# Unit 0, its handover to unit 1, and the last unit rearranged: first keys in three passes, film rows spread by TensorE, low value halves shared

## What is computed

```
xn  = layernorm(x) * ln_w + ln_b
q   = softmax(xn @ Wq + bq, over the features of a head)
k   = softmax(xn @ Wk + bk, masked, over the 512 tokens)
v   = xn @ Wv + bv                      (layer 0: times the mask)
att = k^T v per head;   y = q att
scale, shift = split(silu(emb) @ W_emb + b_emb)      one row per batch
h   = layernorm(y) * ln2_w + ln2_b, then * (1 + scale) + shift
x   = x + silu(h) @ W_out + b_out
```

## Time and profile before

| | |
|---|---|
| median of 3 runs | 791.26 us |
| the profiled execution's own time | 791.3 us |
| its span (first to last instruction) | 789.5 us, mean granted TensorE clock 0.991 |
| PE busy | 756.9 us (96%) |
| DVE busy | 688.4 us (87%) |
| ACT busy | 517.3 us (66%) |
| POOL busy | 444.9 us (56%) |
| DMA | 130.80 MB, mean 166 GB/s |

### The profile page before, as it was taken

How to read it: one execution, slowest core, us unless ns; L and a number is a source line. 1 busy time by engine, 2 the same in 40 slices (tenths; PEclk the granted TensorE clock), 3 DMA queues, 4 the chain that set the end, 5 groups by cost and what they waited for, 6 DMA issues and landing times.

```text
span 789.5 us, 18061 instructions
## 1 busy us (share of the span) xinstructions
PE 756.9 (96%) x6959; PEld 407.3 (52%) x6959; DVE 688.4 (87%) x1413; ACT 517.3 (66%) x1010; POOL 444.9 (56%) x437
## 2 busy tenths in 40 slices
PE   5996979999999999999999999999999999999997
PEld 3445446564464645546464554645455464646443
DVE  6897978789998999999988899988889988888976
ACT  5767585756657687686867676576657566571553
POOL 2356394654846758577664655636354544737253
PEclk9997999999999999999999999999999999999999
DMA  9958897765957659687594939779493959668282
GB/s 329 318 103 196 245 183 207 146 149 151 167 167 156 159 154 187 174 170 192 91 204 121 187 121 172 191 143 188 105 200 108 184 158 160 149 112 184 55 160 81
DMA packets 291510, 130.80 MB, mean 166 GB/s; under 512 B 261728, under 2 KB 262112, under 8 KB 291424
## 3 DMA queue, kind: packets, MB, share of 16 engines
q1 hardware_dynamic: 288688, 125.27, 71.1%
q10 hardware_dynamic: 2736, 4.39, 1.6%
HBM read 47.74 MB, written 16.88 MB: 82 GB/s over the span
## 4 chain that ended last, share of the span: by engine, by line
PE 50%; DVE 28%; ACT 8%; issue 7%; POOL 3%; DMA 3%; SPq 1%; DVEq 0%; ACTq 0%; POOLq 0%
PE ring L540 37%; DVE sb_k_or_qt L1058 5%; PE ring L589 3%; ACT sb_k_or_qt L1443 3%; DVE ring L1146 2%; DVE sb_y_stats L1150 2%; PE att_ps L686 2%; DVE sb_ht_parts L1163 2%; PE ring L595 2%; DVE sb_q_max L1091 2%; DVE ring L1093 2%; DMA sb_k_or_qt<-sb_tanh 2%; DVE ring L1088 2%; DVE sb_ht_parts L1175 2%; PE ring L733 1%
## 5 line engine op out<-in xcount | busy, mean ns | idle before, releaser
L540 PE MATMUL ring<-sb_w_hi,sb_xt_parts 128*128 128x512 f16 x1024 | 309.0, 379 | 0.0
L540 PE MATMUL ring<-sb_w_lo,sb_xt_parts 128*128 128x512 f16 x512 | 194.0, 379 | 0.0
L540 PEld LDWEIGHTS ring<-sb_w_hi,sb_xt_parts 128*128 128x128 f16 x1024 | 100.4, 98 | 123.4 <-issue 3.8
L540 PE MATMUL ring<-sb_w_hi,sb_ht_parts 128*128 128x512 f16 x512 | 155.9, 380 | 2.1 <-issue 1.7
L1709 POOL TENSOR_TENSOR sb_htok<-sb_ht_parts,sb_htok 128x512 f16<-128x512 f32 x60 | 75.3, 1276 | 131.1 <-ACT sb_htok L1480 131.1
L1725 POOL TENSOR_TENSOR sb_tanh<-sb_v_or_q,sb_kq_hi 128x512 f16<-128x512 f32 x64 | 74.2, 1159 | 86.2 <-ACT sb_kq_hi L1520 85.3
L540 PE MATMUL ring<-sb_w_lo,sb_ht_parts 128*128 128x512 f16 x256 | 97.1, 379 | 0.0
L1513 ACT ACTIVATE sb_v_or_q<-ring,sb_ln_one 128x512 f32<-128x512 f32 x64 | 43.9, 686 | 63.9 <-DVE ring L1093 63.9
L1700 POOL TENSOR_TENSOR sb_x<-sb_x,sb_bias_o 128x512 f32<-128x512 f32 x64 | 79.3, 1275 | 6.8 <-DVE sb_w_lo L979 6.8
L540 PEld LDWEIGHTS ring<-sb_w_hi,sb_ht_parts 128*128 128x128 f16 x512 | 50.1, 98 | 61.6 <-issue 2.6
L540 PEld LDWEIGHTS ring<-sb_w_lo,sb_xt_parts 128*128 128x128 f16 x512 | 50.1, 98 | 59.5 <-issue 0.7
(11 more groups left out here) (239 smaller groups left out, 1565.2 us busy)
## 6 DMA issues: line engine op xcount, KB each, us to landing
out<-sb_x SPq DMA_DIRECT2D x14, 1024.0 KB, 5.7
sb_rows_now<-film_rows SPq DMA_DIRECT2D x16, 512.0 KB, 4.6
sb_x<-out SPq DMA_DIRECT2D x8, 1024.0 KB, 5.4
sb_x<-in_x SPq DMA_DIRECT2D x7, 1024.0 KB, 5.5
sb_mask_add<-mask_terms SPq DMA_DIRECT2D x15, 256.0 KB, 6.1
sb_w_hi<-in_L_cond_W_emb SPq DMA_DIRECT2D x1, 1536.0 KB, 14.1
sb_w_lo<-in_L_cond_W_emb SPq DMA_DIRECT2D x1, 1536.0 KB, 14.9
sb_w_hi<-in_L_cond_film_emb_W ACTq DMA_DIRECT2D x1, 1536.0 KB, 7.6
```

Of the source, the lines that this page charges most:

```text
L540: last = nc.tensor.matmul(out, lhs, rhs, start=(n == 0), stop=(n == len(pairs) - 1))
```

## The change

It has these parts.

1. First keys. All four K tiles of unit 0 are made in three passes over the tiles: high*high of all four, then high*low, then low*high; before, two tiles had three passes and two came one after the other. The peak sum of Wk is put between transposes 2 and 3, `first_x_low(0)` ahead of `find_scale(0, K)`. DVE does `find_peak` and `find_scale` of Q and `find_peak` of V ahead of the masked keys; ACT scales Wq ahead of `x_squares(1)`.
2. Values of unit 0. The bound of V is made from the peaks alone (`ln_bias_abs`, `bias_rows`), so that `find_scale(0, V)` gives the final scale; `v_scales(0)` with its reduction is gone. The sums of V's shift move to between Q tiles 1 and 2. DVE does `queries(0, 0)` ahead of `split_low(V)`.
3. Film rows. Unit 0's rows are no longer written to memory and read back before it uses them: PE spreads the two rows with four f32 matmuls of 256 columns (`first_rows`) into ring banks 0 and 1, and ACT copies them into `rows_now`. The table is stored at the head of step 1; no rows are loaded for unit 0. `film_scales` comes ahead of `values(0, 3)` on DVE, `bound_film(0)` is inside V tile 3 on PE. The loading of layer 1's film weights from ACT's queue is split in two: half 0 at the end of unit 0, half 1 after `normalise(2)`.
4. Handover. The first half of K tile 0 of unit 1 (12 matmuls of 256 columns) comes between `first_attention` and `attend(0)`. `find_peak(0, O)` comes ahead of `attended_all(0)`, `sum_w(0, O)` right after `attend(0)`, `find_scale(0, O)` and `output_scale(0)` between the moments and the centring of the first pair of Y. ACT scales Wo at the head of step 1, ahead of the tanh and the key exponents; POOL does `low_weight(0, O)` and then `add_bias(0)` ahead of `low_h(0)`.
5. Last unit. Of the value tiles 2 and 3 the low half is made by DVE (`values(u, 2)`, `values(u, 3)`), and ACT casts them in one step. The `tail` on DVE is one loop over the four tiles, each from `attended` to `affine`; the transposes of h stand at other places between PE's output matmuls.

The core of the diff:

```diff
 (SP)
-                turn_x(0, 1, (0,))
-                store_table(0)
-                turn_x(0, 1, (1,))
+                turn_x(0, 1)
             def step(u):
                 if u == 1:
-                    load_rows(0)
+                    store_table(0)
 (PE)
-            def first_keys(between):
+            def first_keys():
...
+                for i in range(C):
                     for c in range(C):
-                        nc.tensor.matmul(outs[i], hi[:, c, f], xt_lo[:, :, c, :], start=False, stop=False)
+                        nc.tensor.matmul(outs[i], hi[:, c, i * P:i * P + P], xt_lo[:, :, c, :], start=False, stop=False)
+                    if i == 1:
+                        sum_w(0, Q_)
+                for i in range(C):
...
+                    if i == 1:
+                        shift_sums(0, K_)
+                shift_sums(0, Q_)
+                shift_parts(0, V_)
+                sum_w(0, V_)
+            def keys_of_first_half(u, i):
+                hi, lo = w_hi[layer_of(u)][K_], w_lo[layer_of(u)][K_]
+                if u == 1:
+                    pe.wait_ge(first_rows_ready, C)
+                out = take_bank("K", i, u).rearrange("p (t m) -> p t m", t=T)
+                pe.wait_ge(xt_hi_ready, 32 * u - 16)
+                pe.wait_ge(xt_lo_ready, 32 * u - 16)
...
+            def first_rows():
+                pe.wait_ge(film_ready, 1)
+                pe.wait_ge(q_exp, 4)
+                for c in range(C):
+                    at = c % 2 * 2 * P
+                    last = nc.tensor.matmul(ring[c // 2][:, at:at + 2 * P], ident[:, 32 * c:32 * c + 1].broadcast_to([P, P]),
+                                            film[:].rearrange("p n e -> p (n e)"), start=True, stop=True)
+                last.then_inc(first_rows_spread, 1)
...
-                project_tokens("V", 0, V_, xt_hi, xt_lo)
-                bound_film(0)
+                project_tokens("V", 0, V_, xt_hi, xt_lo, (0, 1, 2))
+                project_tokens("V", 0, V_, xt_hi, xt_lo, (3,), at=((4, lambda: bound_film(0)),))
+                first_rows()
                 first_attention()
+                keys_of_first_half(1, 0)
                 attend(0)
+                sum_w(0, O_)
 (DVE, first_unit)
                 find_peak(0, Q_)
+                find_scale(0, Q_)
+                find_peak(0, V_)
                 masked_keys(0, 0)
...
                 key_shift(0)
+                fold(0, Q_)
...
+                key_sums(0)
+                queries(0, 0)
                 split_low(V_)
                 for i in range(C):
                     low_keys(0, i)
+                fold(0, V_)
                 queries(0, 1)
-                v_scales(0)
                 queries(0, 2)
+                queries(0, 3)
                 values(0, 0)
-                queries(0, 3)
+                rows_of_film(0)
+                find_film_peak(0)
                 values(0, 1)
                 values(0, 2)
+                film_scales(0)
+                query_sums(0, (0, 1))
                 values(0, 3)
+                query_sums(0, (2, 3))
+                query_recip(0)
                 dve.wait_ge(blocks_loaded, 16)
                 mask_attention(0)
                 find_peak(0, O_)
...
+                attended_all(0, scales_of_output)
 (ACT, first_unit and step)
-                high_values(0, range(T))
-                x_sums(2, (0, 1))
+                high_values(0, (0,))
+                x_sums(2, (0,))
+                high_values(0, (1,))
+                x_sums(2, (1,))
+                high_values(0, (2,))
+                x_sums(2, (2, 3))
+                high_values(0, (3,))
+                copy_first_rows()
                 high_attention(0)
-                x_sums(2, (2, 3))
                 x_squares(2)
+                load_film_w(1, 0)
...
                 if u == 1:
-                    load_film_w(1)
+                    load_film_w(1, 1)
+                    scale_and_split(0, O_)
                 h_beside_keys(u)
-                if u == 1:
-                    scale_and_split(0, O_)
 (POOL, step)
-                low_h(u - 1)
                 if u == 1:
                     low_weight(0, O_, o0_ready)
+                    add_bias(0)
+                low_h(u - 1)
 (DVE, last unit)
+                values(u, 2)
+                values(u, 3)
                 query_sums(u)
...
+                for t in range(T):
+                    attended(LAST, t)
+                    y_statistics(LAST, t)
+                    y_moments(LAST, (t,))
+                    centre(LAST, t)
+                    if t:
+                        last_h_low(t - 1)
+                    affine(LAST, t)
```

More of the change, by code:

```diff
@@ L885, in wait_here, with power @@
                 nc.vector.memset(spare[:, word:word + 1], 0.0)
-            def power(layer, n):
-                at = (slice(None), layer, slice(n, n + 1))
+            def power(layer, n, end=None, step=1):
+                at = (slice(None), layer, slice(n, n + 1 if end is None else end, step))
                 link(nc.vector.tensor_scalar(scale_down[at].bitcast(I32), peak_all[at].bitcast(I32), EXP_BITS, None, ALU.bitwise_and))
@@ L949, in fold @@
                     bias, shift = (bias_q[layer] if m == Q_ else bias_v)[:], shift_at(layer, m)
+                if (layer, m) == (0, V_):
+                    dve.wait_ge(v_bias_up, 1)
+                    nc.vector.scalar_tensor_tensor(out=bias, in0=shift, scalar=scale_up[:, 0, V_BOUND:V_BOUND + 1], in1=bias, op0=ALU.mult,
+                                                   op1=ALU.add).then_inc(shift_folded, 1)
+                    dve.wait_ge(shift_folded, folded(0, V_))
+                    return
                 nc.vector.tensor_tensor(bias, shift, bias, ALU.add).then_inc(shift_folded, 1)
@@ L1160, in centre @@
             def centre(unit, t):
-                dve.wait_ge(rows_loaded, 16 * (unit + 1))
+                if unit:
+                    dve.wait_ge(rows_loaded, 16 * unit)
+                else:
+                    dve.wait_ge(first_rows_ready, C)
                 in_halves = lambda a: a.rearrange("p (j n) -> p j n", j=2)
@@ L1184, in attended_all @@
                     y_moments(u, pair)
+                    if pair[0] == 0:
+                        between()
                     for t in pair:
@@ L1343, in _ @@
             nc.vector.tensor_copy(mask_cols[:], att_ps[:, 0, 0:B * T]).then_inc(mask_cols_ready, 1)
+            first_x_low(0)
             find_scale(0, K_)
-            for t in range(T):
+            for t in range(1, T):
                 first_x_low(t)
@@ L1546, in h_beside_keys, with copy_first_rows @@
                 high_h(u - 1, 3)
+            def copy_first_rows():
+                act.wait_ge(first_rows_spread, 1)
+                out = rows_now[:].rearrange("p n (j c e) -> p n j c e", j=2, c=C)
+                for c in range(C):
+                    at = c % 2 * 2 * P
+                    nc.scalar.copy(out[:, :, :, c, :], ring[c // 2][:, at:at + 2 * P].rearrange("p (n j e) -> p n j e", n=2, j=2)
+                                   ).then_inc(first_rows_ready, 1)
             def first_unit():
@@ L1744, in first_unit @@
                 x_mean(1)
+                low_weight(0, Q_, q0_ready)
                 x_norm(1)
-                low_weight(0, Q_, q0_ready)
-                pool.wait_ge(w_ready[0], 8)
-                add_bias(0)
                 for t in range(T):
                     low_x(1, t)
+                pool.wait_ge(shift_summed, folded(0, V_))
                 low_queries(0)
-                low_values(0)
+                low_values(0, (0, 1, 2))
+                x_mean(2)
+                low_values(0, (3,))
                 low_attention(0)
-                x_mean(2)
                 x_norm(2)
@@ L1785, in last_unit @@
                 low_h(u - 1)
-                for t in range(T):
-                    low_queries(u, (t,))
-                    low_values(u, (t,))
+                low_queries(u, (0,))
+                low_values(u, (0,))
+                low_queries(u, (1,))
+                low_values(u, (1,))
+                low_queries(u, (2, 3))
                 low_attention(u)
```

174 lines of the change are left out of this document (68 added, 106 removed).

## The result

The changed kernel took 783.45 us (median of 4 runs, 782.83 to 785.27), the kernel before beside it 791.46: ratio 0.9901, 95% interval 0.9889 to 0.9913. That is 8.0 us faster, against 8.8 forecast (782.5), inside the range. A second set of runs of the same kernel, on another occasion, gave 784.37 (783.50 to 785.06), 6.9 us under the kernel before beside it.

What follows compares the result with a forecast made beforehand. PE's own work was taken as the bound. Gains of 8.5 us up to unit 2 and 0.3 in the last unit, together 8.8 off 791.3 us, gave 782.5 us; range 779.5 to 787.5, the forecast's own 779.8 to 785.

Steps and rivals of the forecast that it cites:

- What bounds the kernel: PE's own work, its idle time at most 32.6 us; units 2 to 14 show next to no waits.
- Part 1: Unit 0's first keys: the 1.4 us wait for Wq's peak goes, Q folded at 32.2; gain so far 1.7 us.
- Parts 2 and 3: Unit 0's values and film rows: V ends at 58.95, only 0.5 us earlier; attention ends at 64.7.
- the 1.36 us of a wait: `centre(0, 0)` no longer waits 1.36 us for the DMA of the film rows, since PE spreads them.
- Part 4: Handover through unit 1: unit 2 starts at 115.6 instead of 124.17; gain 8.5 us.
- The cover for `low_weight(0, O)`: Unit 1: ahead of `low_h` it fits POOL's idle time, ending with `add_bias(0)` at 88.5 to 90.
- ScalarE's DMA issue: Handover in unit 1: film load issue may block ACT, at worst 4.6 us at each of two places; 1.6 taken.
- Part 5: Last unit: DVE's chain sets the end, last affine at 780.0 against 780.3; gain 0.3 us.
- A: Rival, chance 0.12: ACT's issue blocks 4.6 us at each half, unit 1's output tiles start at 107.9; 786.6 us.
- B: Rival, 0.12: clock falls around 59 to 64 us, 784 us. As stretch: `key_shift(0)` to masking unit 0's attention.
- C: Rival, 0.04: nothing measurable, 790 to 791.3 us. As stretch: masking unit 0's attention to unit 2's first key matmul.
- D: Rival, 0.05: slower, Wo's scaling ahead of unit 1's exponents becomes a bound; 794.5 us at 17 us of blocking.

Runs made afterwards that it cites:

- c2: Changed kernel with unit 0's film rows spread by DMA again, without PE's spreading matmuls and ACT's copies; 792.69 us, ratio 1.0010.
- b1: Changed kernel plus eight unused matmuls on PE ahead of query tile 1 of unit 1; 783.64 us, ratio 0.9908.
- a2: Changed kernel with `add_bias(0)` left out, so unit 0's output lacks the bias; 780.89 us, ratio 0.9867.
- b3: Changed kernel with `add_bias(0)`'s four tiles moved between the low query tiles of unit 1 on POOL; 780.85 us, ratio 0.9881.
- c3: Changed kernel with its last unit as in the kernel before; 784.47 us, ratio 0.9910.
- a0: The changed kernel run again unaltered, as yardstick; 784.37 us, ratio 0.9910.
- b2: Changed kernel with unit 0's query tile 0 waiting only for the keys' fold, not the queries'; 783.92 us, ratio 0.9914.
- after: Profiled execution of the changed kernel in its first set of runs, the longest of the four; 785.27 us.
- a1: Changed kernel with `add_bias(0)` put back into unit 0, after `x_norm(1)`; 783.57 us, ratio 0.9903.
- a3: Changed kernel with the first half of unit 1's K tile 0 back behind `attend(0)`; 785.15 us, ratio 0.9915.
- c4: Changed kernel with unit 0's keys as before, two tiles in passes, then two whole tiles; 783.76 us, ratio 0.9906.
- b4: Changed kernel with the edits of b2 and b3, plus unit 0's value tile 3 ahead of the query sums on DVE; 781.16 us, ratio 0.9876.

## Why the prediction was right, and where it was not

- *What bounds the kernel.* Right in the main. Most of the gain lies ahead of unit 2. Units 2 to 14 kept their programs and gave 1.05 us more (unit 15 starts 5.68 us earlier, unit 2 4.63), which was not forecast. It is no chance of one execution: from unit 2 to unit 15 it is 600.4 us before and 599.1 to 599.4 in eleven of the thirteen changed ones (c2 600.0, b1 600.7). The differences sit in units 3, 7 and 9 (0.3, 0.5 and 0.4 us), in small waits that "next to nothing" passed over; why they are shorter stays open.
- *Part 1.* `fold(0, Q)` was named rightly as what is late next. It came at 33.7, not 32.2: the scale of Q was done 0.3 us late, and two small steps of Wv's peak beside POOL's `low_weight(0, Q)` took 0.73 and 0.90 us where 0.16 was counted, 1.3 us in all. PE waited 1.9 us where 0.7 had been forecast, and behind that wait the clock fell in this execution: 1.6 us of B.
- *Parts 2 and 3.* Q and V took 27.8 us from 33.87 (26.2 in a2, where the clock stayed full), so V ended at 61.69, 2.7 us after the forecast 58.95. The scaling of the film rows took 0.45 us instead of the 1.24 counted and gave 0.8 back, and unit 0's attention ended at 66.67 instead of 64.7. The 2.0 us missing in unit 0 are these: 1.5 from the late fold and 1.3 more than forecast for Q and V, less 0.8. Rows and copies cost about what was forecast (1.89 us for the four matmuls, which the trace counts as eight, where 1.7 was said, and 1.19 for the copies). What they guard against was not seen: they were credited with the 1.36 us of a wait, and without them the time is 8 us longer (c2), since the weights' load that another part lets go early was not seen as a danger to the rows.
- *Part 4* is the step that failed. "`add_bias(0)`, moved beside unit 1's exponents and low keys, costs DVE between 0 and 4 x 0.39 = 1.6 us there; I take 0.4". It costs 2.5 us (C with and without it; a2 and b3 agree to 0.04), all of it ahead of the low keys, which take 4.17 us for four, against 4.16 before. Two things were wrong. The sum charged the low keys alone, while the instructions in fact beside `add_bias(0)` are two affines (0.72 us more each) and the sum of the keys (1.07 more). And the bound came from a mean that mixes: of the 4.59 us of the four low keys in the earlier trace rows GpSimd stood idle for 2.3, from 42.86 to 45.17. The trace of before already had the price of a small instruction, beside the same `add_bias(0)` in unit 0:

```profile
38.00 1.20 DVE L1049 TENSOR_SCALAR sb_k_sum<-sb_k_sum 128x4 f32<-128x4 f32 x1 [0.18 <-ACT sb_k_or_qt L1443]
```

  By the rule of the Trainium skill (GPSIMD Engine Reference, Specifications) the sum would have been 1.2 us longer, the better choice, though still 0.9 short, as it was priced from the same row.

  The path was wrong as well: the forecast had the exponents of the keys end ScalarE's queue at 85.0, bound by that queue. They waited 2.5 us for DVE's `key_shift` and ended at 88.2. The cover for `low_weight(0, O)` was said to hold; the stretched instructions beside it (0.6, 0.9, 1.0 us over their length with POOL still) come to 2.5 us more; no run took it away, so this is read from rows and not shown. ScalarE's DMA issue, taken at 1.6 us, blocked nothing (issues of 0.37 to 0.61 us). These two went in opposite directions.
- *Part 5.* 0.3 forecast; 0.40 in the first profile, 0.28 by c3 against a0.
- *Rivals.* A did not happen. Its 107.9 also does not follow from the terms given: 9.2 us of blocking behind 101.6 make 110.8, and which part would be hidden is not said. B happened, in two other places: the one in unit 1 was without price (b1, b2), the one in unit 0 was worth 1.6 us in the executions in which it came. Where it had been feared, in waits forecast at 0.5 and 1.8 us and measured at none and 1.2, the clock stayed full. C and D did not happen. That the gain can be used up by a transfer that lands late, as in c2, was among no rivals.

Of the forecast's 8.5 us, 4.6 showed at unit 2 in this profile. From the end of unit 0's attention the forecast had 50.9 us to unit 2 (64.7 to 115.6), and it took 52.9 (66.67 to 119.54). These 2.0 us are about the 2.1 by which `add_bias(0)` was priced too low; that nothing else remains is luck, since the 1.6 for ScalarE's issue and the stretch beside `low_weight(0, O)` cancel in part. The other 2.0 were lost in unit 0. Nor is the nearness of the totals (8.0 us measured, 8.8 forecast) a confirmation of the sum. The profiled execution gained 6.0: 4.6, the unforeseen 1.05, and 0.4 in the last unit; its last affine was done 6.1 us earlier than before (774.2), not 8.5 to 9. The median owes the rest to three executions that were 1.2 to 2.4 us shorter and have no profile; the clock in unit 0 alone is worth 1.6 us between executions of the same code (B).

## What to carry to other kernels

Work moved into an idle stretch of GpSimd is not free if VectorE works out of SBUF beside it: count the instructions there that take two SBUF inputs, and the tensor_scalar on two columns or more, at up to one GpSimd tile each, and try the work where VectorE reads PSUM. A wait removed is worth what comes behind it, so follow the engine that was late before counting the gain. When a load is let go earlier, look for the small latency-bound transfer that now lands behind it.

## What the hardware showed that was not expected

- Beside GpSimd's tensor_tensor of 1.24 us a tile, tensor_tensor and tensor_scalar on 2 to 4 columns on VectorE: 0.16 us alone, 0.73 to 1.23 beside it; 128x512 with operands in SBUF 0.70 to 0.75 alone, 0.99 to 1.72; with one operand in PSUM 0.68 in either case. Some of the stretched (L1077, L908, L909, L951) have a single tensor input. Reductions, the reciprocal and tensor_scalar on one column kept their 0.15 to 0.21 us. GpSimd's own tiles went from 1.24 to 1.58.
- Behind the wait of 1.7 to 1.9 us ahead of query tile 0 of unit 0 the granted clock was 0.79 in 33:41 in seven executions (after, a0, a1, a3, c2, c3, c4) and 1.00 in three (a2, b1, b3). Behind the 2.0 us ahead of query tile 2 of unit 1 it was 0.86 in 96:108 in three (after, a0, c3) and 1.00 in two (b2, c4); behind the 2.0 us ahead of the first film product 0.93 in 36:60 in b2 and 1.00 in b4. Behind the wait of 1.2 us ahead of the last quarter of unit 0's attention it stayed at 1.00 in 60:76 (after, a0); in a3, where a wait of 1.4 us followed, it was 0.79.
- The load of the film rows, 0.5 MB written, took 12.4 us from issue to landing with 2 MB of weights issued 3 us before it, and 4.9 us in the kernel before without them.
